# Expert layer in slots of 256 tokens, with weights stationary in the first product and no transposes between the products

## The reference, cut to what matters

```python
xn = _layernorm(x)                                   # 4096 tokens, width 512
s = _L0_attn_ref(xn, Wqkv, b_qkv, Wout, b_out)       # 16 heads, causal, alibi
logits = x_flat @ w_router.T                         # x_flat is xn, 2 experts
top_idx = jnp.argmax(softmax(logits), axis=-1); top_weight = probs[top_idx]
h = jnp.einsum('nd,ehd->enh', x_flat, w_fc)          # hidden width 2048
a = jnp.square(jnp.where(h >= 0, h, 0.5 * h))
expert_out = jnp.einsum('enh,edh->end', a, w_proj)
g = _silu(expert_out[top_idx] * top_weight)
return x + s * g
```

## Time and profile before

| what | value |
|---|---|
| median of 3 runs | 1679.99 us (1679.72 to 1680.52) |
| span of the profiled execution | 1675.0 us |
| time outside the span, if the profiled execution took the median | 5.0 us |
| first to last matmul of the expert products | 841.8 to 1654.3 us |
| one slot of 128 tokens, steady | 24.12 us |

### The profile page before, as it was taken

How to read it: one execution, slowest core, us unless ns; L and a number is a source line. 1 busy time by engine, 2 the same in 40 slices (tenths; PEclk the granted TensorE clock), 3 DMA queues, 4 the chain that set the end, 5 groups by cost and what they waited for, 6 DMA issues and landing times. The chain is left out here.

```text
span 1675.0 us, 33419 instructions
## 1 busy us (share of the span) xinstructions
PE 1469.1 (88%) x9220; PEld 801.5 (48%) x9221; DVE 1232.2 (74%) x2871; ACT 790.2 (47%) x1944; POOL 669.2 (40%) x893
## 2 busy tenths in 40 slices
PE   3889898979888898988479999999999999999994
PEld 1355555545554555555234444444444444444442
DVE  7699989989998899989386655665666566556655
ACT  3477777867776786878273222222222222212221
POOL 0456555564655456465123233323332332233231
PEclk9989999999999998999789999999999999999998
DMA  3424243343324234232382011101100110111010
GB/s 142 152 83 127 96 146 96 99 130 103 115 95 136 89 103 139 90 108 83 110 308 70 20 39 38 38 19 38 38 27 27 33 38 19 38 38 38 19 32 26
DMA packets 84884, 133.11 MB, mean 79 GB/s; under 512 B 14095, under 2 KB 63247, under 8 KB 82576
## 3 DMA queue, kind: packets, MB, share of 16 engines
q1 hardware_dynamic: 75808, 105.71, 19.5%
q0 software_dynamic: 8944, 25.83, 5.0%
HBM read 97.82 MB, written 33.95 MB: 79 GB/s over the span
## 5 line engine op out<-in xcount | busy, mean ns | idle before, releaser
L1028 PE MATMUL psY<-wf,aT 128*128 x1584 | 363.8, 379 | 27.5 <-DVE aT L1136 23.2
L1002 PE MATMUL psF<-wf,xT 128*128 x1584 | 368.6, 383 | 7.3 <-DVE wf L1113 5.4
L876 POOL TENSOR_SCALAR pr<-pr,rden 128x128 f32<-128x128 f32 (+3 forms) x512 | 262.7, 531 | 178.4 <-DVE rden L804 177.3
L1215 POOL TENSOR_TENSOR a<-a 128x512 f32<-128x512 f32 x132 | 153.1, 1160 | 445.8 <-DVE a L1129 435.8
L1069 ACT ACTIVATE rl<-psF 128x512 f32<-128x512 f32 x132 | 78.7, 596 | 478.0 <-PE psF L1002 478.0
L559 ACT ACTIVATE pr<-pr,mn 128x128 f32<-128x128 f32 (+3 forms) x512 | 283.5, 557 | 0.0
L793 DVE CUSTOM_DVE_ANT_0 pr<-psS,base,nsl 128x128 f32<-128x128 f32 (+3 forms) x512 | 249.6, 543 | 13.8 <-issue 8.9
L434 PE MATMUL psT<-conf,pr 128*128 128x128 f32 x1280 | 214.4, 287 | 49.5 <-POOL pr L876 25.5
L545 ACT ACTIVATE pt<-psT 128x512 f16<-128x512 f32 (+1 forms) x384 | 200.2, 522 | 117.0 <-PE psT L434 110.7
L1028 PEld LDWEIGHTS psY<-wf,aT 128*128 128x128 f16 x1584 | 154.4, 97 | 202.6 <-issue 50.5
L1002 PEld LDWEIGHTS psF<-wf,xT 128*128 128x128 f16 x1584 | 156.1, 99 | 191.2 <-issue 15.3
(11 more groups left out here) (146 smaller groups left out, 1627.4 us busy)
## 6 DMA issues: line engine op xcount, KB each, us to landing
qk_parts<-pre SPq DMA_DIRECT2D x64, 256.0 KB, 2.2
qs<-qk_parts SPq DMA_DIRECT2D x128, 128.0 KB, 2.6
ks<-qk_parts SPq DMA_DIRECT2D x128, 128.0 KB, 2.5
wst<-in_wf SPq DMA_DIRECT2D x16, 1024.0 KB, 5.3
wstage<-in_wf SPq DMA_DIRECT2D x32, 512.0 KB, 5.6
xin<-in_x SPq DMA_DIRECT2D x32, 256.0 KB
attn_out<-so SPq DMA_DIRECT2D x32, 256.0 KB, 2.1
pt<-in_wqkv SPq DMA_DIRECT2D x4, 768.0 KB, 10.1
```

The lines of the kernel that those rows point to most:

```text
L876: nc.gpsimd.tensor_scalar(p_, p_, rden[:, c:c + 1], 32768.0, ALU.mult, ALU.mult).then_inc(s["norm_done"], 1)
L1002: last = nc.tensor.matmul(ps[:], xT[:, r % 2, x, kc * P:(kc + 1) * P], w(e, 2 * hc, hl, kc), start=(k == 0), stop=(k == 3 * KC - 1))
L1028: last = nc.tensor.matmul(psY[r % 2][:], aT[:, hc % 2, x, q * P:(q + 1) * P], w(e, 2 * hc + 1, hl, q), start=(hc == 0 and k == 0), stop=(h ...
L1215: nc.gpsimd.tensor_tensor(at, at, at, ALU.mult).then_inc(s["a_ready"], 1)
```

## The change

Slots have 256 tokens (`TT`), so there are 17. The hidden width goes in 8 groups `c` of 256 (`GR`) instead of 4 of 512. In `up` the weights are stationary (128x128) and 256 tokens move: 24 matmuls for a group, with the result already turned (hidden on partitions). `turn`, its transposes and `psU` are gone; `ahi` (ScalarE) and `alo` (VectorE) make the two float16 parts from `a` in SBUF. `down` makes two halves of 128 tokens: 12 matmuls of 512 columns for a group. `up` runs two groups ahead of `down` (`LEAD`). The work per slot at a slot's end is done for 256 tokens at a time, or in two halves, and it stands at other groups of the step; the last sum is written into `z`, and `ob` is gone. The gathers and scatters are two DMAs per slot each. The `split` calls stand at eight places from group 6 of step -1 to group 4 of step 1, and the ring of `wstage` has 4 buffers.

```diff
-SLOTS = TOK // P + 1
+TT = 256
+SLOTS = TOK // TT + 1
+GR = HID // 256
+LEAD = 2
...
+def ahead_of(n, c, lead):
+    return n + (c + lead) // GR, (c + lead) % GR
-        HP, RING = 1024, 5
+        NH = TT // P
+        HP, RING = 1024, 4
+        def weights_due(n, c):
+            if isinstance(n, int) and (n, c) in ((-1, GR - LEAD), (0, 0), (0, 2), (0, 4), (0, 6), (1, 0), (1, 2), (1, 4)):
+                return n * HC + (c + LEAD) // 2
+            return None
...
+            def up(n, r, c, e):
+                t, hc = n * GR + c, c // 2
+                if c == 0:
+                    wait(pe, s["X_lo"], (n + 1) * NH)
+                if isinstance(n, int) and n < 2:
+                    wait(pe, s["ws_lo"], 2 * (2 * hc + 1 + n * NP))
                 wait(pe, s["f_sum"], t - 1)
+                for k in range(2):
+                    col = (2 * (c % 2) + k) * P
+                    m = 0
+                    for hl, parts in ((0, (0, 1)), (1, (0,))):
+                        for kc in range(KC):
+                            for x in parts:
+                                last = nc.tensor.matmul(psF[c % 2][:, k * TT:(k + 1) * TT],
+                                                        w(e, 2 * hc, hl, kc * 512 + col, P), xT[:, r % 2, x, kc, :],
+                                                        start=(m == 0), stop=(m == 3 * KC - 1))
+                                m += 1
                 last.then_inc(s["F_done"], 1)
-            def turn(n, r, hc):
...
+                wait(pe, s["U_lo"], t + 1)
+                for k in range(2):
+                    q = 2 * (c % 2) + k
+                    for m, (x, hl) in enumerate(((0, 0), (1, 0), (0, 1))):
+                        for h in range(NH):
+                            last = nc.tensor.matmul(psY[r % 2][h][:], aT[:, c % 4, x, k, h * P:(h + 1) * P],
+                                                    w(e, 2 * hc + 1, hl, q * 512, 512),
...
+                for c in range(GR):
+                    nu, cu = ahead_of(n, c, LEAD)
+                    if within(nu, 0, SLOTS):
+                        up(nu, r + (cu < c), cu, e1 if cu < c else e0)
+                    if c in (2, 4) and ahead:
+                        xtrans(n + 1, (c - 2) // 2)
                     if here:
+                        down(n, r, c, e0)
...
+                for c in range(GR):
+                    nh, ch = ahead_of(n, c, 1)
+                    if within(nh, 0, SLOTS):
+                        ahi(nh, ch)
+                    if weights_due(n, c) is not None:
+                        split(weights_due(n, c))
+                    if within(nu, 0, SLOTS):
+                        relu(nu, cu)
+                    if c == 1 and within(n - 1, 0, SLOTS):
+                        wait(act, s["z_ready"], n + 1)
...
+                                             ACT.Exp, scale=-1.0).then_inc(s["g_exp"], 1)
+                    if c in (3, 5) and within(n + 1, 0, SLOTS):
+                        h = (c - 3) // 2
+                        wait(act, s["X_done"], (n + 1) * NH + h + 1)
...
...
+                for c in range(GR):
+                    if done and c == 0:
+                        wait(dve, s["Y_done"], n * GR)
+                        wait(dve, s["out_done"], (n - 1) * 16 * NH)
+                        for h in range(NH):
+                            link(ts(z[:, h, :], psY[rm % 2][h][:], rec[:, rm, h * MROW + 1:h * MROW + 2], x(X_CY),
+                                    ALU.mult, ALU.mult))
+                        ts(flat(gt[:]), flat(z[:]), -80.0, None, ALU.max).then_inc(s["z_ready"], 1)
+                    if within(nh, 0, SLOTS):
+                        alo(nh, ch)
+                    if weights_due(n, c) is not None:
+                        split(weights_due(n, c))
+                    if within(nu, 0, SLOTS):
+                        total(nu, cu)
+                    if done and c in (2, 3):
+                        h = c - 2
+                        if h == 0:
+                            wait(dve, s["g_exp"], n)
+                            link(ts(flat(gt[:]), flat(gt[:]), 1.0, None, ALU.add))
+                        ins = nc.vector.reciprocal(gt[:, h, :], gt[:, h, :])
+                    if done and c == 4:
+                        link(tt(flat(z[:]), flat(z[:]), flat(gt[:]), ALU.mult))
+                        link(tt(flat(z[:]), flat(z[:]), flat(sg[:, rm % 2, :, :]), ALU.mult))
+                    if done and c == 5:
+                        link(ts(miss[:], field(2), eslot[:, bass.ds(n - 1, 1)], float(OOB), ALU.not_equal, ALU.mult))
+                        link(tt(oidx[:], miss[:], field(0), ALU.add))
+                        tt(flat(z[:]), flat(z[:]), flat(xg[:, rm, :, :]), ALU.add).then_inc(s["o_ready"], 1)
+                        dve.wait_ge(s["o_ready"], n)
+                    if c == 0 and within(n + 2, 0, SLOTS):
+                        fetch(n + 2, r + 2)
+                    if c in (1, 3) and within(n + 1, 0, SLOTS):
+                        h, r1 = (c - 1) // 2, (r + 1) % 4
...
+                        ts(xn[:], xg[:, r1, h, :], rec[:, r1, h * MROW + 3:h * MROW + 4],
+                           rec[:, r1, h * MROW + 4:h * MROW + 5], ALU.subtract, ALU.mult).then_inc(s["ln_done"], 1)
+                    if c in (3, 5) and within(n + 1, 0, SLOTS):
+                        h = (c - 3) // 2
+                        wait(dve, s["X_hi"], (n + 1) * NH + h + 1)
...
+                                                       op0=ALU.mult, op1=ALU.subtract).then_inc(s["X_lo"], 1)
```

More of the change, by code:

```diff
@@ L974, in _, with expert @@
         def _(pe):
[L975 to L984, removed]
+            def expert(n):
+                return pe.value_load(eint[0:1, bass.ds(n, 1)], min_val=0, max_val=1)
@@ L1021, in down @@
+            def down(n, r, c, e):
+                t, hc = n * GR + c, c // 2
+                if c == 0:
                     wait(pe, s["z_ready"], n)
-                if isinstance(n, int):
-                    wait(pe, s["ws_lo"], 2 * (2 * hc + 2 + (NP if n > 0 else 0)))
+                if isinstance(n, int) and n < 2:
+                    wait(pe, s["ws_lo"], 2 * (2 * hc + 1 + n * NP) + 1 + c % 2)
                 wait(pe, s["U_lo"], t + 1)
[L1025 to L1031, removed]
+                for k in range(2):
[4 more added lines that the diff above has]
+                                                    w(e, 2 * hc + 1, hl, q * 512, 512),
+                                                    start=(c == 0 and k == 0 and m == 0),
+                                                    stop=(c == GR - 1 and k == 1 and m == 2))
@@ L1056, in split @@
             def split(m):
-                for n in range(m * 4, (m + 1) * 4 if m < E * HC else 0):
+                for n in range(m * 4, (m + 1) * 4):
                     e, q, h = n // (2 * NP), n // 2 % NP, n % 2 * HP
@@ L1070, in relu @@
                                      ).then_inc(s["f_relu"], 1)
[L1072 to L1076, removed]
-            def step(n, r):
[L1079 to L1082, removed]
-                    if here:
-                        uhi(n, r, hc)
-                    if isinstance(n, int) and n in (-1, 0):
-                        split((n + 1) * HC + hc + 1)
-                    if ahead:
-                        relu(n + 1, r + 1, hc)
-                    if hc == 1 and within(n - 1, 0, SLOTS):
-                        wait(act, s["z_ready"], n + 1)
-                        nc.scalar.activation(gt[:], gt[:], ACT.Exp, scale=-1.0).then_inc(s["g_exp"], 1)
-                    if hc == 1 and within(n + 2, 0, SLOTS):
-                        wait(act, s["X_done"], n + 3)
-                        wait(act, s["F_done"], (n + 1) * HC)
-                        nc.scalar.activation(xT[:, r % 2, 0, :], psX[:], ACT.Copy, scale=1024.0
@@ L1199, in _ @@
+                assert not done or k[0] == LK, k[0]
             slots(dve, step)
@@ L1234, in _ @@
-            pool.sem_inc(s["ob_free"], 1)
+                        for h in range(NH):
+                            nc.gpsimd.indirect_dma_start(
+                                out=io["out"], out_offset=bass.IndirectOffsetOnAxis(ap=oidx[:, h:h + 1], axis=0),
+                                in_=z[:, h, :], in_offset=None, bounds_check=TOK - 1, oob_is_err=False
+                            ).then_inc(s["out_done"], 16)
+                    if c == 0 and within(n + 2, 0, SLOTS):
+                        wait(pool, s["idx_ready"], n + 3, s["apart_pool"])
+                        gather(xg[:, (r + 2) % 4, :, :], io["x"], r + 2, x_got[(r + 2) % 4])
@@ L1235, in _ @@
+                    if c == 1 and within(n, 0, SLOTS):
+                        gather(sg[:, r % 2, :, :], io["s"], r, s_got[r % 2])
             slots(pool, step)
-            pool.wait_ge(s["out_done"], SLOTS * 16)
+            pool.wait_ge(s["out_done"], SLOTS * 16 * NH)
 def build(nc, x, wqkv, bqkv, wout, bout, wr, wf, const, out):
```

237 lines of the change are left out of this document (90 added, 147 removed).

## The result

The changed kernel takes 1714.94 us (1712.3 to 1715.96, 4 runs), the kernel before 1679.86 on the same chip: ratio 1.0222, interval 1.0199 to 1.0245. The forecast was slower by 1.1%, 1698 us. The direction held, and so did the places of the forecast waits; the loss is twice the one forecast. The profiled execution took 1715.72 us with a span of 1713.9, so 1.8 us lie outside the span, not 5.0.

A forecast was written before the change was run, and what follows sets the result against it. TensorE bounds the kernel, busy 724.6 of 751 us. First `up` 845.0, work 723.5, splits 39.7, clock 18.0, steady waits 38.6, end 28.8 make 1693.6; plus 5.0 outside the span, say 1698 us; forecast band 1683 to 1717, range 1650 to 1722.

The forecast's parts named there:

- from there to the first `up`: Expert part's start: two gathers, x's preparation at slow clock and the first split put the first `up` at 845.0 us.
- the end: Behind the last `down`: VectorE's closing work for 256 tokens and a second scatter take 28.8 us, against 20.7 before.
- The work on TensorE: All 17 slots: 256-column matmuls cost 0.109 us, stationary loads hidden; 42.56 us a slot, 723.5 us in all.
- Rival B: `up` matmuls: stationary loads show at 256 columns, up to 30 ns each, 50 us, giving 1749 us; chance 0.07.
- The steady slot: Steps 1 to 15: TensorE waits 0.4 us for `xn` and 2.2 for x's low part each, 38.6 us in all.
- The weights' start: First slots: first `up` at 845.0 us, then TensorE waits for split weights at seven places, 39.7 us.
- the clock term of the sum: Start and six of seven split waits: matmuls at 1.2 GHz cost 18.0 us, bounds 2.8 and 20.6.
- rival C: Steady slots: waits of 2.2 us in each slot pull the clock down, 15 x 2.5 more, 1736 us; chance 0.05.
- The point of decision: Whole expert part: waits and clock together, forecast at 96.3 us, must fall under 77.7 for the change to gain.
- high ones 1710: Whole sum: taking all the high bounds was said to give 1710 us.
- sign for rival B: Steady stretch: a step over 46 us with `psF` groups longer than 2.9 would make visible stationary loads right.

The follow-up runs named there:

- the mended kernel: Changed kernel without the loop, splits one group earlier, x's normalised half and low parts earlier in VectorE's queue: 1614.33 us, ratio 0.9623 to the kernel before.
- the one swap: Changed kernel with the low part of x's second half made before the index pair and last sum in group 5: 1663.67 us, ratio 0.9925.

## Why the prediction was right in kind and wrong in size

The sum against the profiled execution, term by term, in the prediction's own order (start to start; a recorded wait begins at the modelled end of the last matmul, 0.17 us after the next could have started, so each counts 0.17 more than its row):

| term | forecast | measured | difference |
|---|---|---|---|
| end of the attention part (first instruction of the expert part, 827.3 before, 831.4 after) | 0 | +4.1 | +4.1 |
| from there to the first `up` | 17.7 | 18.4 | +0.6 |
| TensorE's work, 17 slots | 723.5 | 723.4 (17 x 42.55, in the mended kernel) | -0.1 |
| seven waits for splits | 39.7 | 38.3 (37.1 + 7 x 0.17) | -1.4 |
| clock, start and behind the splits | 18.0 | 15.2 (2.7 + 12.5) | -2.8 |
| waits for x in steps 1 to 15 | 38.6 | 34.4 for the low part, 15 x 0.3 for `xn` | +0.3 |
| clock behind those waits and jumps | 0 | 12.6 | +12.6 |
| jumps of the loop | 0 | 5.4 (5.0 + 2 x 0.17) | +5.4 |
| the end | 28.8 | 29.6 | +0.8 |

These make 19.5 of the 20.3 us between 1693.6 and 1713.9. The 0.8 at the end is a wait that the forecast missed: `ob` is gone, so the last scaling into `z` waits for the scatter before it (1685.27, where the last `down` ended at 1684.27); in the kernel before it began 0.04 behind the `down`.

**The work on TensorE** was right to a hundredth: 0.109 us a matmul with its own stationary load, no transposes, 42.55 us a slot. Rival B is out. So is the Trainium skill's rule that a load overlaps only with matmuls of another row group (TensorE: Matmul & The Clock Gate, "What overlaps and what doesn't"): 3264 full-array loads were hidden behind matmuls of 256 columns, as 24 in 2.78 us show.

**The steady slot** was right in place and size: the wait of 2.15 us for the low part of the second half, once a slot, made by the index pair and the sum beside GpSimd's square, whose length (1.95 for 1.23) was also forecast (1.97). Taking the order away took the wait away.

**The weights' start** was right in its seven places; their lengths, 7.19, 4.48, 4.48, 4.30, 5.58, 4.76 and 6.34, stand beside 7.4, four times 4.85, 5.95 and 6.9. The slow groups behind them cost 1.8 each, 12.5 in all, for the 15.2 forecast.

**The step that failed is the clock term of the sum**, 18.0 us, which held the start and the splits and put the waits of the steady slots at nothing. They were rival C: "waits of 2.2 us in each slot pull it down as the 3.95 did. 15 x 2.5 more", given a chance of 0.05 and left out of the sum. It was taken as all or nothing, and what spoke against it was a row about waits of 0.8 us, a third as long. The runs show a mechanism of degree: 7 of 15 groups behind waits of 2.0 to 2.15 us, 14 of 15 behind 3.1 to 3.4, none behind the 0.8 of the kernel before. It should have stood in the sum as a term from 0 to 24 (15 x 1.6), and nearly half of it was paid: 11.0 us, and 1.5 behind one of the jumps. The price of one is 1.6, not 2.5, since only a part of the group ran at 1.2 GHz: around the one of 1168.21 the mean clock is 0.93 from 1168.0 to 1169.5 us and 0.50 from there to 1172.5.

**The second term that was put at nothing** is the loop. Two jumps back cost 5.4 us and one of the slow groups. The instruction queue of the profile shows what is new about it. Packets, megabytes and share of that queue: in the kernel before none from 1100 to 1500 us, in the changed one
```profile
q8 instruction: 29, 0.48, 0.5%
```
in the same stretch, and two of them lie between 1176 and 1181 us, at the jump. The body of four slots had 464 matmuls with their loads, and now it has 1184; instructions are fetched all through the loop. The Trainium skill (Runtime: NRT & Kernel Launch, "Instruction fetch mechanics") says that a taken branch whose target is not among the pages held stops the engine until the page has come; the trace agrees in place, 2.71 and 2.34 us at the two jumps, and unrolling removed them. Fetching by itself costs TensorE nothing that can be seen: without the loop and with both orders mended, the queue moves as much in the same stretch,
```profile
q8 instruction: 28, 0.46, 0.5%
```
and TensorE has no wait there. A jump without fetching, in the kernel before, costs about 0.5 us. Only where the two come together did it cost 2 to 4 us, in kernels that differ in more than this. That TensorE waits for a page at the jump fits this, but no run shows the single fetch that it waited for.

The 4.1 us of the attention part are no effect of the change as far as these runs go: the profiled executions of the eleven kernels end it anywhere from 823 to 834 us, the smallest for an edit far behind it. And 3.2 us of the forecast came from taking 5.0 us outside the span where it is 1.8. Without this the forecast would have been further off.

The point of decision, "the waits and the clock together must fall under 77.7", can be tested: after the one swap they came to 57 (38.2, 14.3 and 4.6), the jumps with a slow group to 7.6, and 77.7 less 64.7 is 13; measured are 13.8 us (1677.42 to 1663.67).

Two more things in the prediction do not hold. Its "high ones 1710" is not what its own high bounds for the waits and the clock give: 39 for 38.6 and 20.6 for 18.0 make 1702 (the 30 ns a load are rival B's). So 1714.94 lies above what the sum allowed for waits and clock, and that it still falls within 1683 to 1717 is luck. Its sign for rival B, a step over 46 us with `psF` groups longer than 2.9, came out (46.4 us on average from 985 to 1636 us, with groups of 4.05 to 4.46 in it) though B is false: the sign could not tell a visible load from a slow clock. What tells them apart is that the groups without a wait in front stayed at 2.78.

## What to carry to other kernels

When a change makes an engine's steps coarser, write out its queue for one period and look at what stands ahead of the instruction that the bounding engine waits for; here three instructions in the wrong order cost 46 us of a change that saves 72 on TensorE's work. Price a wait on TensorE at its length plus the slow matmuls behind it, with a share of cases that grows with its length. And when a loop's body grows, look whether the instruction queue was silent in the loop before.

## What was not expected of the hardware

- TensorE's granted clock falls behind some waits of 2.0 to 2.15 us (7 of 15), nearly all of 3.1 to 3.4 us (14 of 15), and behind none that were filled with matmuls of no use but for 1.3 us or less; each fall there costs 1.3 to 1.7 us on a group of 2.78.
- Nine useless matmuls in each of 15 waits made the kernel 14 us faster, 12 of them in the section.
- A jump back cost TensorE 2.2 to 4.0 us in these kernels where the instruction queue works all through the loop, and about 0.5 where it is silent there.
- A sum or product of 128x1024 elements from SBUF on VectorE took 1.23 us alone and 1.95 when GpSimd's square had begun before it; where VectorE had begun first (1210.58 for 1210.84 us in the changed kernel) it took 1.21 and the square 1.85 for the usual 1.06.
